# VectorE finishes a weight piece before the low halves of block 1's rows, in the two steps that have both

## What is computed

```python
x = L0_attn_x                                                       # (4, 512, 512) fp32
x = x + 0.5 * ffn(layernorm(x), w_gate_up, w_proj_ffn)              # layer 1
x = x + attention(layernorm(x), w_qkv, w_proj, b_proj)              # layer 2: relu linear attention
x = x + 0.5 * ffn(layernorm(x), w_gate_up, w_proj_ffn)              # layer 3

def ffn(x, w_gate_up, w_proj):
    wq = ternary(w_gate_up)          # bf16; per 64 weights: scale = mean|w|, q = clip(round(w / scale), -1, 1)
    gate, up = split(x @ wq.T)       # hidden size 2048
    h = silu(gate) * up
    return rms_norm(h) @ ternary(w_proj).T
```

## Time and profile before

| | |
|---|---|
| median of 3 runs | 886.41 us (885.18 to 888.3) |
| the profiled execution | 886.26 us |
| its span, first to last instruction | 884.5 us |
| TensorE busy (matmuls) | 868.8 us, 98% of the span |
| VectorE busy | 478.0 us, 54% |
| ScalarE busy | 398.9 us, 45% |
| GpSimd busy | 72.3 us, 8% |
| granted TensorE clock | 1.0 (2.4 GHz) in every slice |

### The profile page before, as it was taken

How to read it: one execution, slowest core, us unless ns; L and a number is a source line. 1 busy time by engine, 2 the same in 40 slices (tenths; PEclk the granted TensorE clock), 3 DMA queues, 4 the chain that set the end, 5 groups by cost and what they waited for, 6 DMA issues and landing times.

```text
span 884.5 us, 12718 instructions
## 1 busy us (share of the span) xinstructions
PE 868.8 (98%) x4864; PEld 403.4 (46%) x4864; DVE 478.0 (54%) x911; ACT 398.9 (45%) x761; POOL 72.3 (8%) x106
## 2 busy tenths in 40 slices
PE   6899999999999999999999999999999999999998
PEld 4644444444444444444444444444444444444445
DVE  7899997924245444518393938543434444433232
ACT  6877667536334445223332425343343443433331
POOL 3211001200010000100000000000000010000000
PEclk9999999999999999999999999999999999999999
DMA  9999708996535687520202010054433343332236
GB/s 291 131 167 134 88 1 159 203 194 138 106 68 128 120 164 161 92 55 1 49 1 43 7 36 14 13 104 67 93 72 72 72 72 72 71 72 60 60 65 138
DMA packets 234827, 80.77 MB, mean 91 GB/s; under 512 B 221200, under 2 KB 224016, under 8 KB 234768
## 3 DMA queue, kind: packets, MB, share of 16 engines
q1 hardware_dynamic: 226144, 66.34, 39.9%
q0 software_dynamic: 3872, 4.72, 4.2%
q10 hardware_dynamic: 4752, 8.91, 3.2%
HBM read 25.43 MB, written 4.19 MB: 33 GB/s over the span
## 4 chain that ended last, share of the span: by engine, by line
PE 92%; DMA 4%; DVE 2%; ACT 2%; issue 1%; ACTq 0%; DVEq 0%
PE proj_ps L1191 23%; PE gate_ps L1177 22%; PE up_ps L1177 22%; PE sum_ps L1312 5%; PE up_ps L1312 5%; PE gate_ps L1312 5%; PE proj_ps L1214 4%; PE proj_ps L1177 3%; DMA att_w<-aw_hl 1%; DMA aw_hl<-in_L_ffn_w_gate_up_dram 1%; DMA slots<-in_L_ffn_w_gate_up_dram 1%; PE gate_ps L1224 1%; PE sum_ps L1163 1%; PE proj_ps L1325 1%; DMA xs<-xn 0%
## 5 line engine op out<-in xcount | busy, mean ns | idle before, releaser
L1191 PE MATMUL proj_ps<-down_w,slots 128*128 128x512 bf16 x928 | 204.4, 379 | 0.0
L1177 PE MATMUL gate_ps<-gu_w,xT 128*128 128x512 bf16 (+1 forms) x896 | 201.4, 368 | 2.8 <-DVE o_buf L1086 1.5
L1177 PE MATMUL up_ps<-gu_w,xT 128*128 128x512 bf16 (+1 forms) x896 | 201.4, 368 | 0.0
L873 DVE SCALAR_TENSOR_TENSOR slots<-up_ps,silu 128x512 f32<-128x512 f32 x117 | 80.9, 691 | 175.4 <-PE up_ps L1177 145.4
L620 ACT ACTIVATE silu<-gate_ps 128x512 f32<-128x512 f32 x117 | 69.0, 590 | 163.5 <-PE gate_ps L1177 163.3
L1191 PEld LDWEIGHTS proj_ps<-down_w,slots 128*128 128x128 f16 x928 | 90.7, 98 | 110.1 <-DVE xs L895 0.8
L1177 PEld LDWEIGHTS gate_ps<-gu_w,xT 128*128 128x128 f16 x896 | 85.4, 98 | 102.4 <-DVE o_buf L1086 1.9
L1177 PEld LDWEIGHTS up_ps<-gu_w,xT 128*128 128x128 f16 x896 | 85.3, 98 | 98.2
L630 ACT ACTIVATE o_buf<-slots 128x512 f32<-128x512 f32 x128 | 80.4, 628 | 97.2 <-DVE slots L873 96.4
L886 DVE SCALAR_TENSOR_TENSOR slots<-slots,inv 128x512 f16<-128x512 f32 x124 | 91.1, 744 | 1.2 <-ACT slots L641 1.1
L641 ACT ACTIVATE slots<-slots,inv 128x512 f16<-128x512 f32 x124 | 86.5, 712 | 7.7 <-POOL inv L548 4.2
(11 more groups left out here) (137 smaller groups left out, 775.2 us busy)
## 6 DMA issues: line engine op xcount, KB each, us to landing
out_dram<-xs SPq DMA_DIRECT2D x15, 256.0 KB, 2.3
slots<-in_L_ffn_w_gate_up_dram ACTq DMA_DIRECT2D x6, 512.0 KB, 7.3
aw_raw<-in_L_attn_w_qkv_dram ACTq DMA_DIRECT2D x12, 256.0 KB, 2.7
xs<-in_L_attn_x_dram SPq DMA_DIRECT2D x2, 1024.0 KB, 8.0
aw_raw<-in_L_attn_w_qkv_dram SPq DMA_DIRECT2D x8, 256.0 KB, 3.2
xs<-in_L_attn_x_dram ACTq DMA_DIRECT2D x1, 1024.0 KB, 11.7
aw_raw<-in_L_ffn_w_gate_up_dram POOLq DMA_DIRECT2D x4, 256.0 KB, 8.1
aw_raw<-in_L_ffn_w_proj_dram POOLq DMA_DIRECT2D x4, 256.0 KB, 6.6
```

The costliest lines, as they stand in the source:

```text
L873: nc.vector.scalar_tensor_tensor(out=h_rows(i, q), in0=bank(up_ps, j), scalar=gu_out(i), in1=silu_rows(j), op0=ALU.mult, op1=ALU.mult).the ...
L1177: mm = nc.tensor.matmul(bank(ps, j)[:, first:first + width], xT(m)[:, t, r, k, :], gu_w[:, k, c:c + width], start=(k + r == 0), stop=(k == ...
L1191: mm = nc.tensor.matmul(proj_ps[:, use % 2, :], h_turned(i)[:, r, j, :], down_w[:, j, :], start=(r + j == 0), stop=(r == 1 and j == HC - 1))
```

## The change

`final_weights(p)` is written ahead of the loop over `x_low(1, t)`. Only steps 4 and 5 have both, so the rows of two steps change places.

```diff
@@ -979,9 +979,9 @@
                     hidden(i, q)
                 if p + 1 < PIECES:
                     difference(p + 1)
+                final_weights(p)
                 for t in new:
                     x_low(1, t)
-                final_weights(p)
                 for q, i in made[2:]:
                     hidden(i, q)
                 if p == PIECES - 2:
```

## The result

The changed kernel takes 888.32 us (median of 20 runs) against 886.43 us before (20 runs): ratio 1.0018, interval 1.001 to 1.0025. That is within the 0.3% that one measurement can tell, but the first median lies outside the forecast range (to 888.0 us), and both intervals exclude no change. The forecast said 0.1 us faster.

What follows compares the result with a forecast made beforehand. TensorE, busy 868.8 of 884.5 us, was taken as the bound, with 1.4 us waiting for tile 2's transposing DMA. Terms -0.60, +0.60 and -0.1 summed to -0.1 us: 886.2 us, median forecast 886.3, range 884.9 to 888.0 us.

Steps and rivals of the forecast that it cites:

- VectorE's order: VectorE, steps 4 and 5: statistics at 38.70, final_weights(5) at 45.01, low half of tile 2 at 45.61 us, before 45.60.
- The cover: VectorE, step 4: the wait for ScalarE's high half hides final_weights(4), ending 0.80 us before the low half may start.
- the `hidden` at which the lead ends: VectorE's wait for ScalarE at 62.65 us: the 0.60 us lead lengthens it from 0.36 to 0.96 us.
- The load of piece 13 waits for the turn of piece 9 and stays at about 43.65 us.: GpSimd's loads: those of pieces 11 and 12 go out 0.60 us earlier, that of piece 13 does not move.
- the term of the transfers: Loads beside tile 2's transposing DMA: 0.6 of 4.9 us of overlap leaves, estimated at -0.1 us.
- Rival C: Shifted loads collide with tile 2's turn: TensorE waits 5.8 us longer, 892 us; chance 0.03.
- one for one: End of tile 2's low half: any change shifts TensorE's 1.4 us wait equally, no gap behind absorbing it.
- Step 5's +0.60: VectorE, step 5: final_weights(5) now runs ahead of tile 2's low half, a loss of 0.60 us.
- step 4's -0.60: VectorE, step 4: final_weights(4) moves into a wait, so step 5 begins 0.60 us earlier, a gain.
- Rival B: A wait in step 5 takes the lead back; tile 2's low half starts at 46.21 us, 887.0 us; chance 0.06.
- Rival A: Loads leave tile 2's turn entirely, landing in 3.3 us: 885.5 us, at best 885.0; chance 0.15.
- T: Experiments' theory: the lead makes piece 11's load collide with piece 9's turn, reaching tile 2's turn through piece 13's load.

Runs made afterwards that it cites:

- e1: Kernel before with final_weights ahead of the low halves in step 4 only, step 5 as before; median 887.37 against 886.68 us, ratio 1.0008.
- e2: Kernel before with final_weights ahead of the low halves in step 5 only, step 4 as before; ratio 1.0013 (1.0001 to 1.0024).
- e15: Same kernel as e2 once more (step 5 alone against the kernel before); ratio 1.0005 (0.9994 to 1.0016).
- e8: Kernel before with the loads of pieces 11 and 12 right behind that of piece 10; median 885.75 us, ratio 0.9995.
- e11: Changed kernel with the loads of pieces 11 and 12 right behind that of piece 10; median 885.64 us, ratio 0.9993.
- e16: Same kernel as e11 once more, for more times; median 886.64 us, ratio 0.9996.
- e9: Kernel before, unchanged, profiled a second time; that execution took 887.85 us.
- e3: Kernel before with GpSimd's load of piece 11 ahead of the reciprocal root of tile 2; median 888.78 against 886.68 us, ratio 1.0024.
- e7: Same kernel as e3, a second look; its profiled execution took 888.91 us.
- e4: Changed kernel with the load of piece 11 behind the reciprocal root of tile 3, that of piece 12 right after; median 887.6 us, ratio 1.0004.
- e17: Kernel before with the load of piece 11 alone right behind that of piece 10; ratio 1.0001 (0.999 to 1.0011).

## Why the prediction was wrong

**Right: VectorE's order, to 0.01 us.** The gap in step 4 takes `final_weights(4)`, step 5 begins 0.60 us early, and the low half of tile 2 starts where it did. The cover was thinner than forecast: `difference(5)` ran 0.84 us late in this execution, so 0.44 us of idle time remained before the low half of tile 0 and not 0.80. What was forecast of the waits at other places held too, but for the `hidden` at which the lead ends.

**Wrong: "The load of piece 13 waits for the turn of piece 9 and stays at about 43.65 us."** This is the step that failed. The next sentences did see that the load of piece 11 moves deeper into the turn of piece 9, bounded the delay by 0.6 us, the size of the shift, and left it out of the sum. The turn grew by 1.9 us, three times the shift, and the load of piece 13 moved by 2.0. A shift of one transfer does not bound what it does to another: between 0.8 and 0.2 us of distance the turn changes from 3.2 to 5 us.

**Wrong in sign: the term of the transfers.** It was -0.1 us, from loads that leave the turn of tile 2. The profiles show +0.6 us (0.2 to 0.9), from one that arrives in front of it. Rival C named the collision but looked for it at the turn of tile 2 alone, argued that the loads move away from it, and gave it 0.03.

**Wrong: "one for one".** Step 5's +0.60 and step 4's -0.60 were taken as losses and gains of the end. By e1, e2 and e15 neither is: 0.6 us early brought nothing, 0.6 us late cost nothing in two profiles. The chain of waits goes through the low half since that released the DMA, but the DMA's own time changed the other way: 5.4 us instead of the changed kernel's 4.4 to 4.9 when it was issued early, 3.5 and 3.3 instead of the 4.0 to 4.2 of the kernel before when it was issued late. The Trainium skill ("DMA: Bandwidth & Descriptors", section "Issuing engines are not separate DMA queues") says that transfers from all issuing engines interleave on the same 16 DMA engines, and the rows agree: a load from GpSimd lengthens a turn from SyncE from 3.2 to 5.1 us.

**Rival B** asked for a wait within step 5; there was none. **Rival A** is what e8, e11 and e16 build on purpose: when both loads are gone the turn of tile 2 takes 3.3 to 3.6 us, and the pair comes 0.4 to 0.9 us sooner behind the turn of tile 0.

**Open.** The collision accounts for 0.6 us in the profiles and the medians differ by 1.4 and 1.9. By the last column of the table the rest must lie before tile 2's first pair as well. Part of it is which executions were profiled: the six of the changed kernel and the three of the kernel before have the same mean time, 887.1 us. The start of the turn of piece 9, which scatters from 40.0 to 42.0 us over all kernels, was earlier in the six, and only the distance from it shows the 0.6 us.

The granted clock sorts the executions further. e9, the kernel before once more, has a mean of 0.99; its TensorE waited 2.47 us for ScalarE's |w| up to 33.95 us, and then the clock was 0.50 (1.2 GHz) to 37 us. That stretch begins ahead of the first instruction that the edit moves. Its row: length, busy time of TensorE (matmuls, weight loads), VectorE, ScalarE and GpSimd, then granted clock, DMA share and GB/s.

```profile
34.00:37.00 3.00, 3.00 (x20) 2.17 (x21) 1.71 (x4) 1.98 (x3) 0.00 (x0) 0.50 0.71 89
```

The profile of e2, also 0.99, has the same behind a wait of 2.19 us; no other profile has it, though e1 waited 2.13 us there. Timed executions with a mean clock of 0.99 or less, or 0.998, took 888.5 us in the kernel before (21 of the 117 with a clock on record) and 888.9 in the changed one (11 of 36), in the mean; 8 and 2 more, at 0.994 or 0.996, are counted nowhere. Which of clock and delay causes the other is not shown. Those at 0.992 or 1.0 have these means:

| kernel | executions | mean time |
|---|---|---|
| before | 88 | 886.5 |
| changed | 23 | 887.5 |
| step 4 alone (e1) | 10 | 887.4 |
| step 5 alone (e2, e15) | 15 | 886.8 |
| load early (e3, e7) | 4 | 887.3 |
| load late (e4) | 6 | 886.5 |
| loads first (e8, e11, e16) | 28 | 886.0 |
| before, load 11 first (e17) | 8 | 886.1 |

The grouping was made afterwards and mixes several sets of timings. It says that at like clock the change costs about 1.0 us (95% interval 0.6 to 1.3), that step 4 alone, which has the same collision, costs 0.9 (0.5 to 1.4), and that the changed kernel with the load late shows no cost (-0.5 to 0.5). That is what T says. What lies between these 1.0 us and the 0.6 of the profiles, and why the changed kernel has more executions of the longer kind, stays open. e7 shows that this window can cost 1.5 us rather than 0.6, but in a neighbour of the changed kernel.

## What to carry to other kernels

When an edit moves an instruction, list who is released by it on other queues, and ask what each released transfer will then lie beside; the transfer that matters may be one that no engine was waiting for, two steps ahead of the one in the chain. The size of the shift bounds nothing here: a shift of 0.6 us made the transfer 1.9 us longer. And before an order is worked out to 0.01 us, test whether the end follows it: moving one instruction by 0.6 us in either direction (e1, e2) could have shown here that it does not.

## What the runs showed of the hardware

- The transposing DMA of piece 9 from SyncE's queue landed after 3.1 to 3.2 us when a 256 KB load from GpSimd was issued 0.8 us or more behind it, after 4.4 to 4.9 us at 0.5 us, and after 4.9 to 5.2 us at 0.2 us.
- The transposing DMA of tile 2, issued 0.3 to 1.6 us behind the load of piece 13, let TensorE start 5.4 to 5.7 us behind that load's issue in eight of nine profiles, nearly whatever its own start was. In all nine it landed 0.9 to 1.2 us behind that load.
- In the profiled executions the whole scatter of the time, 885.04 to 888.91 us, lies ahead of tile 2's first pair at 49 to 53 us; the other 835.6 us repeat to within 0.04 us.
- TensorE's granted clock was 0.50 from 34 to 37 us in two of 19 profiles, behind waits of 2.19 and 2.47 us, and executions of the kernel before with a mean clock of 0.99 or less, or 0.998, were 2.0 us longer in the mean than those at 0.992 or 1.0.
